# Seven eighths of the attention layer's output product moved into the scan layer's turns, with four transpose banks and another order of transposes

## The chip, the cores and the metric

One core of a Trainium2 chip. The metric is the device time of one execution in microseconds, here the median of three runs. Engines are named as the profile does: PE is TensorE, DVE VectorE, ACT ScalarE, POOL GpSimd, SP SyncE (here it only issues DMAs).

## The reference

```python
# layer 0, for each of 8 batches (1024 rows of 512), 8 heads of 64
xn = _ln(x, ln_w, ln_b)
q = softmax over a head's 64 of (xn @ Wq + bq)
k = softmax over the 1024 rows of (xn @ Wk + bk + (1 - mask) * -1e6)
v = (xn @ Wv + bv) * mask
att = einsum('bnhd,bnhl->bhdl', k, v)
y = einsum('bnhd,bhdl->bnhl', q, att)
hh = _ln(y, ln2_w, ln2_b) * (1 + scale) + shift
x1 = x + silu(hh) @ W_out + b_out
# layer 1: modulated layer norm of x1, rows gathered by an index, a selective
# scan (state size 16, inner width 1024), gated, projected, rows put back
out = x1 + gate * y1
```

The index is below 512 for every row, so the scan layer reads only the first 512 rows (four tiles of 128) of each batch; the other four tiles of x1 only go to the output.

## The kernel before

Two layers run one after the other, each a block in which every engine has its own list of instructions, tied by semaphores. All matmuls are float32.

**The attention layer** (`layer0`) is a pipeline over batches: `body(b, prev, cur, more)` runs for b = 0 to 8, does the first half of batch b and the second half of batch b - 1. TensorE's order in a body is: y product (attention matrix times Q, L672), z transposes (`turn`, L660), K products, V products (`product`, L652), y transposes, Q products, output product (L652, 8 tiles of 128 rows, each four matmuls), Q transposes, K transposes, and the K-V product that gives the attention matrix (L732). Products go round four PSUM banks (`MM_RING`), transposes round two (`TR_RING`); the K-V product has bank 6. `mm_use` and `tr_use` count the uses of the two rings, so that a wait for the fourth or second use before the next can be written as a constant. ScalarE copies z (L749), exponentiates K (L752), turns y into h by Silu (L764), exponentiates Q (L769), copies Q (L774) and multiplies K by the mask (L779). VectorE adds biases, takes maxima and sums, normalizes z and y (L273), and adds the output product to x (`res`, L888); the rows of x1 then go to DRAM. GpSimd takes the power for the norms, adds the output bias to `res` (L796) and shifts Q by its maximum (L806). Body 8 also does three small products (L284) for the modulation of the next layer, and gathers the next layer's first rows. The attention layer ends when the last stores have landed.

**The scan layer** (`layer1`) has eight turns of 32 units, one a batch; a unit is one of 16 states for half of the inner width, and has four blocks (128 blocks a turn). Per block ScalarE makes a decay (L1523) in one of three banks, VectorE scans it (L1863), TensorE transposes a tile of a finished unit into one of two state banks (L1301), and VectorE adds it, scaled, to a sum (L1881); the fourth tile goes by ScalarE (L1539) and an accumulating DMA of GpSimd's (L1742). GpSimd makes a unit's four inputs in one instruction (L1704), in a ring of four, up to four units ahead. All other work of a turn (transposes, the input product `project_in` L1264, the projections L1275 and L1290, the output product L1349, and what ScalarE and VectorE do with each) stands at blocks written out by hand: `XM_AT`, `Z_AT`, `DT_AT`, `Y_AT` and the like give the block n of a turn at which TensorE's list has it. A product is cut into pieces of one or two of its four matmuls, one piece a block (`ROWS_SPLIT`). These jobs go round three work banks; `batch_places` numbers the uses. SP issues the loads in the same written-out way by unit s, among them one of B (`b_wide`, L1079) per unit, three units early. GpSimd's list has gathers, accumulates and the final additions of y by unit. The last batches' stores are arranged apart.

In `both_chunks` stands a second version for indices of 512 and more, which doesn't run here.

## Time and profile before

| | us |
|---|---|
| median of three runs | 3349.63 (3346.01 to 3351.81) |
| the profiled execution's own time | 3346.66 |
| its span, first to last instruction | 3344.9 |
| mean granted clock of TensorE | 0.915 |
| PE busy | 2824.3 (84%) |
| DVE busy | 2437.0 (73%) |
| ACT busy | 1603.8 (48%) |
| POOL busy | 1838.8 (55%) |

The page's second part shows the span in 40 slices of 83.6 us, a digit for the busy tenths. The first fifteen or so are the attention layer, the rest the scan layer: PE stands at 9 in the first and at 7 to 8 in the second, DVE at 3 to 4 and at 9. The granted clock is a share of full speed, and has two levels, 0.5 (1.2 GHz) and 1.0 (2.4 GHz); a number in between is a mean over a stretch. Groups and waits name the tiles as written by the program, out<-in, and in brackets the idle time of the engine just before and what ended it.

### The profile page before, as it was taken

How to read it: one execution, taken by the hardware profiler on the slowest of the kernel's cores; microseconds unless marked ns; L12 is line 12 of the kernel's file. 1: busy time of each engine (PE TensorE's matmuls, PEld its weight loads, DVE VectorE, ACT ScalarE, POOL GpSimd, SP SyncE). 2: the span in 40 equal slices, each digit the busy share in tenths (PEclk: the TensorE clock that was granted, in tenths of full speed). 3: DMA queues.
4: the chain of work that ended last, by engine and by line, in shares of the span. 5: the costliest groups of instructions: out<-in, count | busy, mean ns of one | idle time of the engine just before them, and what ended most of it. 6: DMA issues, size and time to landing. Idle time of an engine off the chain costs nothing. (4 is left out here: it accounts for less than half of the span.)

```text
span 3344.9 us, 33056 instructions
## 1 busy us (share of the span) xinstructions
PE 2824.3 (84%) x11066; PEld 1589.4 (48%) x11066; DVE 2437.0 (73%) x3146; ACT 1603.8 (48%) x2280; POOL 1838.8 (55%) x801
## 2 busy tenths in 40 slices
PE   7999999999999998678788788787787787787874
PEld 3545454545545443435544445445445444444542
DVE  3444444444444343899999999999999999999994
ACT  1122221222212123657767667667667667667561
POOL 0111111111121110878869969969979979879992
PEclk9999999999999999688798898898897898998976
DMA  5002020211102123344345445455456455455563
GB/s 194 7 26 82 0 82 0 82 42 39 56 25 82 38 79 100 81 95 91 93 114 136 112 118 127 114 123 132 108 123 139 105 125 135 101 131 128 131 154 70
DMA packets 216344, 310.97 MB, mean 93 GB/s; under 512 B 19373, under 2 KB 85041, under 8 KB 216202
## 3 DMA queue, kind: packets, MB, share of 16 engines
q1 hardware_dynamic: 164584, 217.10, 20.7%
q0 software_dynamic: 48064, 91.25, 15.6%
q8 instruction: 71, 1.16, 0.1%
q10 hardware_dynamic: 3554, 0.88, 0.1%
q14 instruction: 71, 0.58, 0.1%
HBM read 200.88 MB, written 42.22 MB: 73 GB/s over the span
## 5 line engine op out<-in xcount | busy, mean ns | idle before, releaser
L1704 POOL TENSOR_TENSOR hs<-slots,b_wide 128x2048 f32<-128x2048 f32 x256 | 1230.0, 4818 | 296.6 <-PE bank L1301 233.8
L1863 DVE TENSOR_TENSOR_SCAN hs<-bank,hs 128x512 f32<-128x512 f32 x1024 | 1219.7, 1208 | 51.8 <-ACT bank L1523 47.1
L1301 PE MATMUL bank<-ident,hs 128*128 128x128 f32 x4096 | 729.3, 310 | 401.8 <-DVE acc L1881 298.8
L1523 ACT ACTIVATE bank<-dt,decay 128x512 f32<-128x512 f32 x1024 | 699.0, 691 | 575.4 <-DVE hs L1863 573.6
L1301 PEld LDWEIGHTS bank<-ident,hs 128*128 128x128 f32 x4096 | 534.0, 158 | 915.0 <-DVE acc L1881 333.0
L1881 DVE SCALAR_TENSOR_TENSOR acc<-bank,c_t,acc 128x512 f32<-128x512 f32 x772 | 560.0, 725 | 28.3 <-PE bank L1301 27.4
L1264 PE MATMUL bank<-h_t,w_in 128*128 128x512 f32 x1024 | 512.9, 608 | 1.0 <-ACT h_t L1457 1.0
L1742 POOL DMA_DIRECT2D acc<-scaled x252 | 270.7, 1074 | 25.8 <-DMA acc<-scaled 23.3
L793 POOL TENSOR_TENSOR y_rs<-y_var,mhalf 128x8 f32<-128x8 f32 x8 | 16.0, 2006 | 440.4 <-DVE y_var L267 440.4
L1349 PE MATMUL bank<-w_y,zs 128*128 128x512 f32 x512 | 253.8, 602 | 0.8 <-DVE zs L1982 0.8
L652 PE MATMUL bank<-z_t,w_k 128*128 128x512 f32 x512 | 221.8, 594 | 5.9 <-ACT z_t L749 5.9
L652 PE MATMUL bank<-w_out,h_t 128*128 128x512 f32 x512 | 221.1, 592 | 0.0
L652 PE MATMUL bank<-rows,z_t 128*128 128x512 f32 x512 | 221.1, 592 | 0.0
L652 PE MATMUL bank<-w_v,z_t 128*128 128x512 f32 x512 | 221.0, 592 | 0.0
L801 POOL TENSOR_TENSOR x_rs<-x_var,mhalf 128x8 f32<-128x8 f32 x7 | 11.5, 1647 | 366.9 <-DVE x_var L267 366.9
L1264 PEld LDWEIGHTS bank<-h_t,w_in 128*128 128x128 f32 x1024 | 171.2, 196 | 84.0 <-issue 84.0
L1539 ACT ACTIVATE scaled<-bank,c_t 128x512 f32<-128x512 f32 x252 | 169.9, 674 | 29.6 <-PE bank L1301 15.6
L806 POOL TENSOR_TENSOR qy<-qy,q_top 128x512 f32<-128x512 f32 x64 | 68.8, 1075 | 200.6 <-DVE q_top L876 200.6
L1831 DVE SCALAR_TENSOR_TENSOR slots<-bank,taps,slots 128x511 f32<-128x511 f32 (+2 forms) x192 | 142.1, 740 | 22.7 <-ACT slots L1463 20.1
L652 PEld LDWEIGHTS bank<-z_t,w_k 128*128 128x128 f32 x512 | 96.6, 190 | 126.4 <-issue 124.5
L652 PEld LDWEIGHTS bank<-w_out,h_t 128*128 128x128 f32 x512 | 97.2, 190 | 122.8 <-issue 122.8
L652 PEld LDWEIGHTS bank<-w_v,z_t 128*128 128x128 f32 x512 | 97.3, 190 | 122.5 <-issue 122.5
(157 smaller groups left out, 3127.8 us busy)
## 6 DMA issues: line engine op xcount, KB each, us to landing
b_wide<-b_rows SPq DMA_DIRECT2D x256, 256.0 KB, 3.5
acc<-scaled POOLq DMA_DIRECT2D x252, 256.0 KB, 4.9
w_in<-in_L_cond_W_in SPq DMA_DIRECT2D x128, 256.0 KB, 3.2
z<-in_x SPq DMA_DIRECT2D x8, 2048.0 KB, 8.5
res<-in_x SPq DMA_DIRECT2D x8, 2048.0 KB, 8.7
x_rows<-res SPq DMA_DIRECT2D x7, 2048.0 KB, 7.4
fin<-x_rows SPq DMA_DIRECT2D x48, 256.0 KB, 4.5
out<-fin SPq DMA_DIRECT2D x48, 256.0 KB, 2.0
```

The costliest lines, as they stand in the source:

```text
L652: last = nc.tensor.matmul(out[:, :], stationary(k), moving(k), start=(k == 0), stop=(k == blocks - 1))
L806: nc.gpsimd.tensor_tensor(heads, heads, q_top[:, t, :].unsqueeze(2).to_broadcast([P, HEADS, HEAD]), ALU.add).then_inc(q_shifted, 1)
L1264: last = nc.tensor.matmul(work_bank(place, stage, m)[:, :], w_in[:, m % W_IN_RING, k, :], h_t[:, place.par, k, :], start=(k == 0), stop=(k ...
L1301: last = nc.tensor.transpose(bank[:, j * P:(j + 1) * P], hs[:, slot, j, t * P:(t + 1) * P], ident[:, :])
L1349: last = nc.tensor.matmul(work_bank(place, "out", t)[:, :], zs[:, j, t * P:(t + 1) * P], w_y[:, j, :], start=(j == 0), stop=(j == KI - 1))
L1523: nc.scalar.activation(decay_banks[N % 3][:, :], dt[:, H % 2, j, :], ACT.Exp, scale=g.decay[:, 4 * (H % 2) + j, s:s + 1]).then_inc(da_read ...
L1539: nc.scalar.activation(scaled[:, U % SCALED_RING, t - DVE_TILES, :], state_banks[t % 2][:, :], ACT.Copy, scale=c_t[:, U // UNITS % 2, t, U ...
L1704: nc.gpsimd.tensor_tensor(hs[:, U % RING, :, :], slots[:, H % SLOTS, :, :], b_wide[:, U % B_RING, :].unsqueeze(1).to_broadcast([P, 4, CHUNK]),
L1742: nc.gpsimd.dma_start(acc[:, U // STATE % 2, DVE_TILES:, :], scaled[:, U % SCALED_RING, :, :], accum_op=ALU.add).then_inc(state_pooled, DMA)
L1831: nc.vector.scalar_tensor_tensor(row[:, back:], bank[:, 0:CHUNK - back], w, row[:, back:], ALU.mult, ALU.add).then_inc(empties(place, "xm" ...
L1863: nc.vector.tensor_tensor_scan(block, decay_banks[N % 3][:, :], block, 0.0, ALU.mult, ALU.add).then_inc(scanned, 1)
L1881: nc.vector.scalar_tensor_tensor(part, state_banks[t % 2][:, :], scale, part, ALU.mult, ALU.add).then_inc(summed, 1)
```

## The change

What it does, in both layers:

- In the attention layer the output product stays for tiles 0 to 3 of batches 0 and 1 alone. For all other tiles h is stored to DRAM (`store_h`, four DMAs for each half of a batch, pieces of 512 bytes) and the rows stored as x1 are x plus bias without the product.
- The scan layer's turns 0 to 6 each compute eight of the 56 tiles: SP loads a tile of h (256 KB, ring of three) by `H_IN_AT`, TensorE multiplies in two pieces of two matmuls at the blocks of `W_AT` (the last at block 130, which is block 2 of the next turn), ScalarE copies the bank to SBUF six blocks later (`keep_w`), and GpSimd adds pairs of tiles (512 KB) to x1 in DRAM by an accumulating DMA at the units of `ADD_W_AT` (37 is unit 5 of the next turn). Turn b does the last four tiles of batch b and the first four of batch b + 2; readers of x1 wait for the pair (`w_landed`).
- Transposes of the attention layer go round four banks instead of two, and the K-V product goes to bank 3.
- TensorE's order in a body is now: z transposes, y product, K, V, y transposes, Q, kept output tiles, K transposes, Q transposes, K-V product. ScalarE's K multiplies stand among the exponentials of Q (`K_BEHIND_Q`).
- Bodies 1 to 3 are written out instead of looped, SP's all of them. SP loads the last batch's rows of x at the end of body 7, and GpSimd adds the bias to them there. The small products of body 8 use banks 0 to 3 and wait for the y product's banks to be empty.
- The gather of the scan layer has one x1 tensor for each batch, and GpSimd's eight small index additions go.

```diff
+ROWS_KEPT = NT // 2
+BATCHES_KEPT = 2
+TR_FIRST = {"z": 0, "k": 8, "q": 16}
 TR_USES = 4 * NT
-TR = {"z": 0, "y": 8, "q": 16, "k": 24}
+TR = {"z": 0, "y": 8, "k": 16, "q": 24}
 TR_LAST = {"y": 0}
-MM_RING, TR_RING = 4, 2
+MM_RING, TR_RING = 4, 4
+K_BEHIND_Q = ((), (), (), (), (), (0, 1), (2, 3), (4, 5, 6, 7))
...
+W_RING = 3
+W_TURNS = BATCH - 1
...
+ADD_W_AT = (7, 30, 32, 37)
+H_IN_AT = (-1, 2, 5, 7, 24, 27, 30, 31)
+W_AT = (7, 11, 89, 101, 106, 110, 121, 130)
...
+W_SPLIT = ((0, 1), (2, 3))
...
+def w_tile(w):
+    b, i = w // NT, w % NT
+    if 2 <= i < 6:
+        return (b + 2, i - 2) if b < BATCH - 2 else (BATCH - 1, i + 2)
+    return b, i + 4 if i < 2 else i
+W_TILES = [w_tile(w) for w in range(NT * W_TURNS)]
...
+            for i in range(NT):
+                if n == W_AT[i] and b < W_TURNS:
+                    use(b, "W", i)
+                if n == W_AT[i] - BLOCKS and 0 < b <= W_TURNS:
+                    use(b - 1, "W", i)
...
+    g.x1 = [scratch(f"x1_rows{i}", [SEQ, DIM]) for i in range(BATCH)]
+    g.h_dram = scratch("h_tiles", [BATCH, NT, P, DIM])
...
+        g.w_out = sb("w_out", [P, KD, DIM])
...
+            def store_h(b, half):
+                need(sp, tr_empty, tr_use(b + 1, "y") + 4 * half + 4)
+                for k in range(KD):
+                    sp.dma_start(h_tiles[b, k][:, 4 * half:4 * half + 4, :],
+                                 h_t[:, k, half * 512:(half + 1) * 512].rearrange("p (t c) -> p t c", c=P)).then_inc(h_stored, DMA)
...
-                if prev:
+                if prev and cur:
                     sp.dma_start(res[:, :, :], batch(x_rows, b - 1)).then_inc(res_loaded, DMA)
...
+                if prev:
+                    need(sp, res_ready, NT * b)
+                    if rows_kept(b - 1):
+                        store_rows(b - 1, slice(ROWS_KEPT, NT))
+                    else:
+                        store_rows(b - 1, slice(0, NT))
+                        store_h(b - 1, 0)
+                    store_h(b - 1, 1)
+                    if rows_kept(b - 1):
+                        need(sp, mm_empty, mm_use(b, "W") + ROWS_KEPT)
+                        store_rows(b - 1, slice(0, ROWS_KEPT))
+                    sp.wait_ge(x1_stored, DMA * stores_of_rows(b))
+                if cur and not more:
+                    sp.dma_start(res[:, :, :], batch(x_rows, b)).then_inc(res_loaded, DMA)
                     sp.wait_ge(mm_ready, mm_use(b, "Q") + NT)
...
+                    sp.wait_ge(tr_ready, tr_use(b, "k") + NT)
+                    sp.wait_ge(kv_ready, b + 1)
+                    load_ada(2)
...
                     sp.wait_ge(gate_stored, DMA)
-                    sp.wait_ge(x1_stored, DMA * (b - 1 + NT // 2))
-                elif prev:
-                    need(sp, mm_empty, mm_use(b, "W") + NT)
-                    sp.sem_inc(passed, 1)
-                    sp.dma_start(batch(x1_rows, b - 1), res[:, :, :]).then_inc(x1_stored, DMA)
-
-                    need(sp, x1_stored, DMA * b)
-                    sp.sem_inc(passed, 1)
+                    sp.wait_ge(h_stored, DMA * halves_of_h(b) * KD)
...
+                if cur:
+                    n = tr_use(b, "z")
+                    for half in range(2):
+                        need(pe, z_ready, NT * (b - 1) + 4 * half + 4)
+                        for i in range(KD):
+                            turn(n, 4 * half + i, [z[:, 4 * half + j, i * P:(i + 1) * P] for j in range(4)])
...
+                    need(pe, tr_empty, tr_use(b, "z") + NT)
...
+                    need(pe, mm_empty, mm_use(b, "y") + NT)
...
+                if prev and rows_kept(b - 1):
+                    need(pe, tr_empty, tr_use(b, "y") + 4)
                     pe.wait_ge(w_out_loaded, DMA)
                     n = mm_use(b, "W")
-                    for t in range(NT):
+                    for t in range(ROWS_KEPT):
                         product((n, t), lambda k: h_t[:, k, t * P:(t + 1) * P], lambda k: g.w_out[:, k, :], KD)
                 if cur:
+                    n = tr_use(b, "k")
+                    need(pe, k_exp_ready, KD * b + KD)
+                    for t in range(NT):
+                        turn(n, t, [k_t[:, i, t * P:(t + 1) * P] for i in range(KD)])
                     n = tr_use(b, "q")
                     for half in range(2):
                         need(pe, q_exp_ready, NT * b + 4 * half + 4)
                         for i in range(KD):
                             turn(n, 4 * half + i, [qy[:, 4 * half + j, i * P:(i + 1) * P] for j in range(4)])
-                    n = tr_use(b, "k")
-                    need(pe, k_exp_ready, KD * b + KD)
-                    for t in range(NT):
-                        turn(n, t, [k_t[:, i, t * P:(t + 1) * P] for i in range(KD)])
-
-                    need(pe, tr_empty, n + NT)
+                    need(pe, tr_empty, tr_use(b, "k") + NT)
                     need(pe, att_ready, 2 * b)
+                    need(pe, mm_empty, mm_use(b + 1, "y"))
                     for i in range(KD):
...
                 if prev:
                     need(act, mod_ready, b)
+                    need(act, h_stored, DMA * KD * halves_of_h(b - 1))
...
+                    n = tr_use(b, "k")
+                    need(act, mask_cur_ready, b + 1)
                     for t in range(NT):
                         need(act, q_shifted, NT * b + t + 1)
                         nc.scalar.activation(qy[:, t, :], qy[:, t, :], ACT.Exp).then_inc(q_exp_ready, 1)
+                        for i in K_BEHIND_Q[t]:
+                            need(act, tr_ready, n + i + 1)
+                            nc.scalar.mul(k_exp[:, i, :], bank(i)[:, :], mask_cur[:, i:i + 1]).then_inc(tr_empty, 1)
...
-                    n = tr_use(b, "k")
-                    need(act, mask_cur_ready, b + 1)
-                    for t in range(NT):
-                        need(act, tr_ready, n + t + 1)
-                        nc.scalar.mul(k_exp[:, t, :], bank(t)[:, :], mask_cur[:, t:t + 1]).then_inc(tr_empty, 1)
...
-                    for t in range(NT):
-                        nc.gpsimd.tensor_tensor(res[:, t, :], res[:, t, :], g.out_bias[:, :], ALU.add).then_inc(res_ready, 1)
+                    if cur:
+                        add_out_bias(b)
...
+                if cur and not more:
+                    add_out_bias(b + 1)
...
                     normed(nc, z, x_mv, x_rs, z_ready)
-                if prev:
+                if prev and rows_kept(b - 1):
...
+        def w_landed(eng, b, t):
+            if (b, t) in W_TILES:
+                q = w_pair(b, t)
+                need(eng, w_added[q % 2], DMA * (q // 2 + 1))
...
+            def load_next_h(w):
+                if w < len(W_TILES):
+                    place, i = w_place(w - W_RING)
+                    load_h(w, filled_by(place, "W", i))
...
+                    for i, at in enumerate(H_IN_AT):
+                        if s == at % UNITS:
+                            w = NT * (b - at // UNITS) + i
+                            if w >= W_RING:
+                                load_next_h(w)
...
+            def project_w(place, i, w, ks):
+                if ks[0] == 0:
+                    claimed(pe, place, "W", i)
+                    need(pe, h_loaded[w % W_RING], DMA * (w // W_RING + 1))
+                for k in ks:
+                    last = nc.tensor.matmul(work_bank(place, "W", i)[:, :], h_in[:, w % W_RING, k, :], g.w_out[:, k, :], start=(k == 0), stop=(k == KD - 1))
+                if ks[-1] == KD - 1:
+                    last.then_inc(fills(place, "W", i), 1)
 
...
+            def keep_w(place, i, w):
+                src = filled(place, "W", i)
+                q = w // 2
+                need(act, w_added[q % 2], DMA * (q // 2))
+                nc.scalar.copy(w_part[:, q % 2, w % 2, :], src[:, :]).then_inc(empties(place, "W", i), 1)
 
...
+                        if n == W_AT[i] + 6 and b < W_TURNS:
+                            keep_w(place, i, NT * b + i)
+                        if n == W_AT[i] + 6 - BLOCKS and 0 < b <= W_TURNS:
+                            keep_w(PLACES[b - 1], i, NT * (b - 1) + i)
...
-            def next_rows(b):
-                need(pool, g.rows_loaded, CT * DMA * (b + 1))
-                nc.gpsimd.tensor_scalar(g.idx_in[:, :], g.idx_in[:, :], SEQ, None, ALU.add).then_inc(idx_in_ready, 1)
+                for t in range(CT):
+                    w_landed(pool, b, t)
+                gather_rows(nc, g, g.x1[b][0:CHUNK, :], g.idx_first, 0)
+            def add_w(q, first, second):
+                for place, i in (first, second):
+                    need(pool, *read_by(place, "W", i))
+                b, t = W_TILES[2 * q]
+                nc.gpsimd.dma_start(x1_tiles[b][t:t + 2].rearrange("t p d -> p t d"), w_part[:, q % 2, :, :], accum_op=ALU.add).then_inc(w_added[q % 2], DMA)
 
             def gather_on(it, b, c):
...
+                    for i, at in enumerate(ADD_W_AT):
+                        q = NT // 2 * (b - at // UNITS) + i
+                        if s == at % UNITS and 0 <= q < len(W_TILES) // 2:
+                            add_w(q, w_place(2 * q), w_place(2 * q + 1))
```

## Rows read from the trace of the kernel before

**Rows 1.** The page's part 5, costliest groups: the output product.

```profile
L652 PE MATMUL bank<-w_out,h_t 128*128 128x512 f32 x512 | 221.1, 592 | 0.0
```

**Rows 2.** Windows: us, busy of PE PEld DVE ACT POOL, PEclk, DMA share, GB/s.

```profile
240.00:480.00 240.00, 229.78 (x873) 126.66 (x872) 104.49 (x190) 50.77 (x82) 36.38 (x30) 1.00 0.16 56
...
2000.00:2300.00 300.00, 244.36 (x1048) 141.42 (x1047) 286.24 (x325) 213.86 (x300) 256.70 (x100) 0.90 0.53 123
```

**Rows 3.** Timeline, TensorE, one batch: start us, us, engine, line, operation, tiles, count.

```profile
528.45 1.04 PE L660 MATMUL bank<-ident,qy 128*128 128x128 f32 x8
...
534.13 27.63 PE L652 MATMUL bank<-rows,z_t 128*128 128x512 f32 x64
561.60 27.63 PE L652 MATMUL bank<-w_out,h_t 128*128 128x512 f32 x64
...
589.07 1.04 PE L660 MATMUL bank<-ident,qy 128*128 128x128 f32 x8
...
600.66 7.41 PE L732 MATMUL bank<-values,k_exp 128*128 128x128 f32 x64 [0.78 <-ACT k_exp L779]
...
622.19 18.29 PE L652 MATMUL bank<-z_t,w_k 128*128 128x512 f32 x42 [0.75 <-ACT z_t L749]
```

**Rows 4.** Timeline of the same batches, ScalarE, GpSimd and VectorE.

```profile
446.25 1.27 ACT L779 ACTIVATE k_exp<-bank,mask_cur 128x512 f32<-128x512 f32 x2 [0.26 <-PE bank L660]
...
563.29 1.34 POOL L806 TENSOR_TENSOR qy<-qy,q_top 128x512 f32<-128x512 f32 x1 [2.39 <-DVE q_top L876]
...
563.22 4.44 DVE L273 TENSOR_SCALAR z<-z,x_mv,x_rs 128x512 f32<-128x512 f32 x8
...
564.66 0.63 ACT L769 ACTIVATE qy<-qy 128x512 f32<-128x512 f32 x1 [3.10 <-POOL qy L806]
...
589.70 1.07 ACT L774 COPY q_t<-bank 128x512 f32<-128x512 f32 x2 [24.41 <-PE bank L660]
```

**Rows 5.** Timeline, TensorE, the first batch.

```profile
138.77 1.04 PE L660 MATMUL bank<-ident,qy 128*128 128x128 f32 x8
...
154.30 7.41 PE L732 MATMUL bank<-values,k_exp 128*128 128x128 f32 x64 [0.78 <-ACT k_exp L779]
```

**Rows 6.** Timeline, all engines, the way out of the attention layer.

```profile
1198.17 7.41 PE L732 MATMUL bank<-values,k_exp 128*128 128x128 f32 x64 [0.78 <-ACT k_exp L779]
...
1213.91 7.03 PE L284 MATMUL bank<-z,cond_t 128*8 128x512 f32 x16
...
1230.18 2.97 ACT L764 ACTIVATE h_t<-bank,mod_cur 128x512 f32<-128x512 f32 x4
...
1273.43 0.37 SPq L630 DMA_DIRECT2D x_rows<-res  x1
1276.70 1.66 DVE L2022 TENSOR_SCALAR d_diag<-ident,cols 128x128 f32<-128x128 f32 x8 [3.29 <-PEq L524]
```

**Rows 7.** Groups by line, 1400 to 3200 us: busy, mean ns, idle before and releaser.

```profile
L1704 POOL TENSOR_TENSOR hs<-slots,b_wide 128x2048 f32<-128x2048 f32 x237 | 1139.9, 4823 | 228.5 <-PE bank L1301 227.2
...
L1863 DVE TENSOR_TENSOR_SCAN hs<-bank,hs 128x512 f32<-128x512 f32 x946 | 1126.9, 1208 | 43.0 <-ACT bank L1523 43.0
...
L1881 DVE SCALAR_TENSOR_TENSOR acc<-bank,c_t,acc 128x512 f32<-128x512 f32 x710 | 515.0, 725 | 24.4 <-PE bank L1301 24.3
...
L1742 POOL DMA_DIRECT2D acc<-scaled x237 | 253.3, 1069 | 25.1 <-DMA acc<-scaled 23.3 <-issue 1.6
...
L1475 ACT COPY zs<-bank 128x512 f32<-128x512 f32 x64 | 37.2, 581 | 12.3 <-PE bank L1264 12.3
```

**Rows 8.** Windows and timeline in the first part of a scan turn.

```profile
2336.20:2400.00 63.80, 48.25 (x223) 32.67 (x223) 58.66 (x70) 45.44 (x66) 59.57 (x27) 0.79 0.53 118
...
2380.43 5.52 POOL L1704 TENSOR_TENSOR hs<-slots,b_wide 128x2048 f32<-128x2048 f32 x1
...
2392.29 2.32 DVE L1863 TENSOR_TENSOR_SCAN hs<-bank,hs 128x512 f32<-128x512 f32 x2
```

**Rows 9.** DMA issues, 1400 to 3300 us: count, KB each, us to landing.

```profile
acc<-scaled POOLq DMA_DIRECT2D x248, 256.0 KB, 4.9
```

More of the change, by code:

```diff
@@ L784, in _, with add_out_bias @@
         def _(pool):
+            def add_out_bias(stores):
+                need(pool, res_loaded, DMA * stores)
+                for t in range(NT):
+                    nc.gpsimd.tensor_tensor(res[:, t, :], res[:, t, :], g.out_bias[:, :], ALU.add).then_inc(res_ready, 1)
             def body(b, prev, cur, more):
@@ L1798, in both_chunks @@
             def both_chunks():
+                for q in range(len(W_TILES) // 2):
+                    add_w(q, (w_first, 2 * q), (w_first, 2 * q + 1))
+                pool.wait_ge(rows_copied, DMA * BATCH)
                 def body(b):
```

168 lines of the change are left out of this document (99 added, 69 removed).

## The prediction

> **What bounds the kernel now.** I read the busy time by stages first [rows 2]. The kernel has two halves with different limits. In the attention half TensorE is busy 229.8 of 240 us at the full clock while VectorE is busy 104.5, so there time is TensorE's work. In the scan half VectorE is busy 286 of 300 us and TensorE 244, so there TensorE work is mostly hidden and VectorE's waits are the price list. The output product is 512 matmul records, 221.1 us [rows 1], 27.6 us a batch, and it stands in the first half. Then I read TensorE's order of work in one batch [rows 3] with the short steps of the other engines around it [rows 4], the first batch [rows 5], the way out of the attention half [rows 6], and for the scan half the idle time ahead of each group [rows 7].
>
> A change under 0.2% (7 us) can't be told from none here.
>
> **Part 1: what leaves the attention half.** 56 of 64 output tiles leave it. Call E the end of the Q products; in [rows 3] it is 561.60. Before: the output product fills 27.5 us, then Q and K transposes with two banks, and the K-V product starts at 600.66, E+39.1.
>
> After, in a batch with no output product, K transposes come at once (K was exponentiated long before). ScalarE's line decides: bank 0 is readable 0.63 us after a transpose starts (589.07 to 589.70) [rows 3, 4]; two K multiplies take 1.27, one exponential 0.63, two Q copies 1.07 [rows 4]. So E+0.6; K0, K1 to 1.9; exponential 6 to 2.5; K2, K3 to 3.8; the last exponential, whose input GpSimd ends at E+3.0 (563.29 + 1.34), to 4.4; K4 to K7 to 7.0; the first four Q copies to 9.1. TensorE's last Q turn waits for the fourth of these (four banks), takes 0.52 and lets the K-V product start at about E+10. Gain 29.1 us. VectorE's two sets of eight passes (normalizing z, 4.4 us from 563.22 [rows 4], then the Q sums, about as long) end near E+11, ahead of the K-V product's end at E+17.4, and cost nothing; were they late, they would hold the attention matrix and so the y product.
>
> Where half the product is kept (two batches) 13.7 us of this stay: gain 15.4. The first batch has no output product: 15.5 us between its Q products and its K-V product [rows 5] become 10, gain 5.5.
>
> From the K-V product's end (608.07) to the K product's start (622.19) are 14.1 us [rows 3]: a wait for the attention matrix, the y product (64 records like the K-V product's, 7.4), z turns, a wait for the last copy. With z turns first the first wait lies behind them and the last behind the y product: about 4.2 + 7.3 = 11.5. Gain 2.6. The y turns took 5.7 us (528.45 to 534.13). With four banks the last one starts after the fourth Silu, 0.64 + 4 x 0.74 [rows 6], so 4.1: gain 1.5. Both seven times.
>
> The way out: 71.1 us from the last K-V product's end (1198.17 + 7.41) to the first VectorE work of the scan half (1276.70) [rows 6]. After: 8.4 to the end of the y product, 0.9 for VectorE's last read of a bank (a new wait; such a read is 0.73 in [rows 7]), 14.1 for two modulation products, 2.2 to the first Silu (1213.91 + 14.1 to 1230.18). TensorE's y turns end near 29.1; then 0.7 for the small turns, 7.0 for the third product, 1.2 to the gate's store, and from the issue of a last store to the next half 3.3 as before (1273.43 to 1276.70): 41.3. Gain 29.8. The new stores of h are ready first: last Silu at 31.6, four issues of 0.4, 4.9 to land [rows 9], 38.1.
>
> Sum: 5.5 + 2 x 15.4 + 5 x 29.1 + 7 x 4.1 + 29.8 = **240.3 us** off the first half, 193.5 of it moved matmuls (7/8 of 221.1), the rest waits. Bounds: without any gain from order and banks only the matmuls go, 193; if TensorE's own 16 turns of 0.52 (8.3 us) set the K-V product's start, 1.7 more in each of eight batches, 254. I stay at 240 because every step of it has a row.
>
> The added transfers of this half (2 MB of h a batch, in pieces of 512 bytes) go beside it: no engine waits for them within 100 us. If that cover went, the wait would be ScalarE's before Silu. Unrolled bodies and a later load of the last rows of x cost nothing: POOL and SP have nothing else then.
>
> **Part 2: what the scan half pays.** Seven turns of 32 units each take eight tiles. Per turn:
> - TensorE: 27.6 us of matmuls at full clock, in pieces of 1.7 us. VectorE now waits for TensorE 24.3 us in 7.4 turns (237 units, 32 a turn) [rows 7], 3.3 a turn. A piece adds its 1.7 to a block of VectorE's of 1.9 (a scan 1.21, an add 0.73), with two state banks between the engines, so it hides at full clock where TensorE idled. The granted clock was 0.79 in the first 64 us of a turn [rows 8], so partly the 1.2 GHz level, and three tiles stand there: six pieces of 3.4 us. Bounds: below zero, -2 (clock comes up, existing waits shrink), above +10 (six pieces 1.7 us longer). I take +1.5, nearest to today's waits.
> - ScalarE: eight copies of 0.58 [rows 7] = 4.6 us. VectorE waits for ScalarE 43.0/7.4 = 5.8 us a turn, in bursts; six of the eight copies fall where ScalarE idles, two beside the table loads. Bounds 0 and 4.6; I take +1.0.
> - GpSimd: four accumulating DMAs to DRAM of 512 KB. No row has that transfer; an accumulating one of 256 KB into SBUF takes 1.07 us of issue [rows 7] and 4.9 to land [rows 9]. Three of four are issued at the start of a turn, where GpSimd is busy 59.6 of 63.8 us [rows 8]. Its lead over VectorE is smallest there: input 8 ends at 2385.95 (2380.43 + 5.52), its scan starts at 2392.29, 6.3 us [rows 8]. Three issues take 3.2; each can delay the next accumulate by up to 4.9. Bounds 0 and 3.2 + 14.7 - 6.3 = 11.6; I take +1.5, because the lead covers all issues and half the delays.
> - SP: eight loads of 256 KB a turn, each waiting for a matmul three tiles earlier; behind it wait loads of B, issued three units (over 20 us) early. Nothing.
>
> Together 4.0 a turn, **+28 us**; bounds -14 and +183, the upper only if all ends meet.
>
> On the DMA the Trainium skill (DMA: Bandwidth & Descriptors, Anatomy of one DMA) gives a GpSimd-issued transfer 2.0 us plus bytes over 436 GB/s. By it 256 KB are 2.6 us, where this trace has 4.9; for 512 KB it would say 3.2, and then the GpSimd term would be nothing. The measured one decides.
>
> Sum against the profiled execution: 3346.66 - 240.3 + 28 = 3134.4. That execution is 3.0 us under the median of the three runs (3349.63), so **3137 us**.
>
> **Rivals.**
> A. GpSimd becomes the bound at the start of each turn (0.10). For it: the lead of 6.3 us. Against: 228 us of its idle time in the rest. Near the bound of 11.6 a turn instead of 1.5: +71, 3208.
> B. The added matmuls bring TensorE's clock up where it was 0.79, and the scan half isn't longer: -1 a turn, 3137 - 28 - 7 = 3102 (0.14). For it: over all stages of a turn the clock is 0.90 [rows 2], so it is higher where more full-size matmuls stand. Against: the low stretch also holds small matmuls and waits that stay. The Trainium skill (TensorE: Matmul & The Clock Gate, What's actually happening) says the gate is released by sustained activity, which is this mechanism; the trace agrees in that low stretches stand where TensorE waits.
> C. The attention half falls short (0.06): another engine's line shows up once the output product is gone, and only the 193 us of matmuls go: 3137 + 47 = 3184.
> D. Slower than before (0.03): accumulating into DRAM reads and writes it, and each of the four waits in GpSimd's queue. GpSimd idles 228.5/7.4 = 31 us a turn; the gain is 240.3/7 = 34 a turn; so it decides from (31 + 34)/4 = 16 us each. At four times the 4.9 us [rows 9] (twice the bytes, twice the traffic) it is 19.6: (78 - 31) x 7 = +329, so 3349.6 - 240.3 + 329 = 3438.
> E. A queue order or a wait undoes the move, and the time stays within 0.2% (0.01).
>
> **How the numbers follow.** The forecast has 0.66. Its own range is a first-half gain of 230 to 250 with 1 to 9 us a turn in the second: 3107 to 3183. The range takes in B's 3102 and most of C: **3098 to 3190**, leaving out A's upper part, D and E, and half of B's tail. Faster by over 0.2%: all but D and E, 0.96; same 0.01; slower 0.03.
>
> **What would show it.** In the profile after: the attention half ends (first VectorE work of the scan half) near 1036 instead of 1277. The K-V product starts about 10 us after the last Q product, 24 in two batches; from one K product's start to the next are 29.1 + 4.1 = 33.2 us less than before. The output product has 64 records at its old line and 448 at a new one. A turn of the scan takes 4 us more; VectorE's idle time ahead of scans and sums grows from 9.1 us a turn to about 13, by ScalarE and TensorE. Wrong would be: a wait for GpSimd's inputs ahead of the scans (A), a granted clock near 1.00 throughout and no longer turns (B), TensorE idle over 3 us ahead of the K-V or y product (C), GpSimd waiting for its new DMAs (D).

## The result and the profile after

| | before | after |
|---|---|---|
| median, us | 3350.07 (3346.01 to 3351.81) | 3134.01 (3131.16 to 3136.52) |
| the profiled execution's own time | 3346.66 | 3136.52 |
| its span | 3344.9 | 3134.7 |
| first VectorE work of the scan half | 1276.70 | 1019.67 |
| scan half (the rest of the span) | 2068.2 | 2115.0 |
| mean granted clock | 0.915 | 0.942 |

The medians are over four executions each; the 3349.63 above was over three of the four before. The scan half is the span less the start of its first VectorE work, the attention half what stands ahead of it.

The ratio is 0.9355 [0.934, 0.937]: 6.45% faster. The forecast was 3137. The sum is right to 3 us, but that is luck: it is made of two errors that cancel. The attention half came out 257.0 us shorter (forecast 240.3), the scan half 46.8 us longer (forecast 28).

The group of the moved matmuls on the page after (line, engine, operation, tiles, count, busy, mean ns, idle before and its releaser):

```profile
L1399 PE MATMUL bank<-w_out,h_in 128*128 128x512 f32 x448 | 234.2, 649 | 1.3 <-ACT dt L1647 1.3
```

The output product has 448 records at its new line [rows 1]. Its mean is 649 ns where the old line had 592 at the full clock: some of the moved matmuls run in stretches of low clock.

TensorE's timeline of one batch after, the stretch that answers to [rows 3]:

```profile
510.75 2.78 PE L719 MATMUL bank<-ident,k_t 128*128 128x128 f32 x24
...
519.65 7.31 PE L793 MATMUL bank<-values,k_exp 128*128 128x128 f32 x64
526.79 3.66 PE L719 MATMUL bank<-ident,z 128*128 128x128 f32 x32
530.29 7.31 PE L737 MATMUL bank<-att,q_t 128*128 128x128 f32 x64
537.43 27.63 PE L711 MATMUL bank<-z_t,w_k 128*128 128x512 f32 x64
...
592.37 4.13 PE L719 MATMUL bank<-ident,qy 128*128 128x128 f32 x32
596.34 27.63 PE L711 MATMUL bank<-rows,z_t 128*128 128x512 f32 x64
...
650.50 4.89 PE L711 MATMUL bank<-z_t,w_k 128*128 128x512 f32 x11
```

The Q products end at 510.75. The K-V product starts 8.9 us later (519.65), the y product follows the z transposes with no wait, and from K product to K product are 650.50 - 537.43 = 113.07 us where 148.77 stood before.

VectorE's groups over five turns of the scan half, first before, then after (the shape group of `slots` and smaller ones left out). The windows run from one early operation of a turn (the first of `h_t`) to the same one five turns on, 1230.03 and 1267.31 us, so a turn went from 246.0 to 253.5 us:

```profile
L1863 DVE TENSOR_TENSOR_SCAN hs<-bank,hs 128x512 f32<-128x512 f32 x640 | 762.6, 1208 | 30.5 <-ACT bank L1523 30.5
L1881 DVE SCALAR_TENSOR_TENSOR acc<-bank,c_t,acc 128x512 f32<-128x512 f32 x481 | 349.0, 726 | 18.5 <-PE bank L1301 18.4
...
L334 DVE TENSOR_SCALAR var<-mv 128x4 f32<-128x4 f32 x5 | 10.9, 2178 | 0.2
...
L340 DVE SCALAR_TENSOR_TENSOR shift<-mv,rs 128x4 f32<-128x4 f32 x5 | 2.2, 437 | 1.9 <-POOL rs L320 1.9
```

```profile
L2029 DVE TENSOR_TENSOR_SCAN hs<-bank,hs 128x512 f32<-128x512 f32 x641 | 763.9, 1208 | 28.0 <-ACT bank L1673 28.0
L2047 DVE SCALAR_TENSOR_TENSOR acc<-bank,c_t,acc 128x512 f32<-128x512 f32 x481 | 349.5, 727 | 38.2 <-PE bank L1435 37.2 <-issue 0.2
...
L371 DVE SCALAR_TENSOR_TENSOR shift<-mv,rs 128x4 f32<-128x4 f32 x5 | 22.3, 4467 | 4.2 <-POOL rs L351 4.2
...
L365 DVE TENSOR_SCALAR var<-mv 128x4 f32<-128x4 f32 x5 | 2.8, 560 | 0.2
```

Three things moved. VectorE's waits for TensorE ahead of the sums went from 18.4 to 37.2 us, 3.8 us a turn. Its waits for ScalarE ahead of the scans went from 30.5 to 28.0. And `shift`, an operation on four numbers a partition, went from 437 to 4467 ns. Together with `var` (2178 to 560 ns) and the wait ahead of it (1.9 to 4.2) that is (20.1 - 8.1 + 2.3)/5 = 2.9 us a turn, of which the prediction has nothing.

The cause of the longer `shift` can be read off GpSimd's and VectorE's timelines at that point. Before, at one turn's start, GpSimd:

```profile
2356.50 1.68 POOL L320 TENSOR_TENSOR rs<-var,mhalf 128x4 f32<-128x4 f32 x1
2358.26 0.25 POOL L1671 TENSOR_SCALAR idx_in<-idx_in 128x8 int32<-128x8 int32 x1
2358.59 4.54 POOL L1704 TENSOR_TENSOR hs<-slots,b_wide 128x2048 f32<-128x2048 f32 x1
```

and VectorE:

```profile
2358.21 0.16 DVE L340 SCALAR_TENSOR_TENSOR shift<-mv,rs 128x4 f32<-128x4 f32 x1 [0.56 <-POOL rs L320]
```

After, GpSimd, and then VectorE:

```profile
2373.45 1.66 POOL L351 TENSOR_TENSOR rs<-var,mhalf 128x4 f32<-128x4 f32 x1
2374.48 5.09 POOL L1866 TENSOR_TENSOR hs<-slots,b_wide 128x2048 f32<-128x2048 f32 x1
```

```profile
2375.14 4.46 DVE L371 SCALAR_TENSOR_TENSOR shift<-mv,rs 128x4 f32<-128x4 f32 x1 [1.63 <-POOL rs L351]
```

Before, the small index addition stood between the power (`rs`) and the making of a unit's inputs, and VectorE's shift, released by the power, ran beside it in 0.16 us. With the addition gone, GpSimd goes straight on into the inputs, and shift ends with that instruction, at 2379.6. The Trainium skill (SBUF — State Buffer, Who interferes with whom) says that a VectorE instruction with two SBUF inputs contends with a GpSimd instruction that reads SBUF, by a lock held for the whole instruction, and that the one that starts second blocks; `shift` has two such inputs (`mv`, `rs`), and the rows agree.

### The profile page after: what moved, and what is told of

It reads as the page before. It is cut to its first block and busy times, and to the rows that moved or that the text cites. A ratio compares the mean times of both kernels' runs of the same rounds, so it can differ in the third digit from the quotient of the medians.

```text
span 3134.7 us, 32596 instructions
## 1 busy us (share of the span) xinstructions
PE 2724.0 (87%) x11066; PEld 1530.8 (49%) x11066; DVE 2404.3 (77%) x3090; ACT 1615.8 (52%) x2336; POOL 1868.2 (60%) x821
## 5 line engine op out<-in xcount | busy, mean ns | idle before, releaser
L1435 PE MATMUL bank<-ident,hs 128*128 128x128 f32 x4096 | 681.1, 294 | 310.4 <-DVE acc L2047 240.8
L1435 PEld LDWEIGHTS bank<-ident,hs 128*128 128x128 f32 x4096 | 507.1, 150 | 848.0 <-DVE acc L2047 319.5
L2047 DVE SCALAR_TENSOR_TENSOR acc<-bank,c_t,acc 128x512 f32<-128x512 f32 x772 | 560.9, 727 | 62.7 <-PE bank L1435 60.6
L1399 PE MATMUL bank<-w_out,h_in 128*128 128x512 f32 x448 | 234.2, 649 | 1.3 <-ACT dt L1647 1.3
L868 POOL TENSOR_TENSOR x_rs<-x_var,mhalf 128x8 f32<-128x8 f32 x7 | 11.5, 1647 | 330.8 <-DVE x_var L298 330.8
L813 ACT ACTIVATE k_t<-k_t,k_top 128x1024 f32<-128x1024 f32 x32 | 36.8, 1149 | 250.0 <-DVE k_top L915 250.0
L1997 DVE SCALAR_TENSOR_TENSOR slots<-bank,taps,slots 128x511 f32<-128x511 f32 (+2 forms) x192 | 142.1, 740 | 22.4 <-ACT slots L1613 19.9
```

The source lines that it names most:

```text
L1399: last = nc.tensor.matmul(work_bank(place, "W", i)[:, :], h_in[:, w % W_RING, k, :], g.w_out[:, k, :], start=(k == 0), stop=(k == KD - 1))
L1435: last = nc.tensor.transpose(bank[:, j * P:(j + 1) * P], hs[:, slot, j, t * P:(t + 1) * P], ident[:, :])
L1997: nc.vector.scalar_tensor_tensor(row[:, back:], bank[:, 0:CHUNK - back], w, row[:, back:], ALU.mult, ALU.add).then_inc(empties(place, "xm" ...
L2047: nc.vector.scalar_tensor_tensor(part, state_banks[t % 2][:, :], scale, part, ALU.mult, ALU.add).then_inc(summed, 1)
```

## The experiments

Each median is over four executions; the kernel before was timed beside each set of runs and stayed within 3350.1 to 3350.8. "Scan half" is that of the profiled execution, as in the table above. It moves by up to 5 us between kernels whose scan layers are the same (2110.6 in e9, 2114.8 in e10, 2115.7 in e5), so a difference of 4 us in it is no more than a hint.

| run | median, us | scan half starts | scan half |
|---|---|---|---|
| changed kernel | 3134.01 | 1019.67 | 2115.0 |
| e1_idx_add | 3115.79 | 1019.84 | 2095.0 |
| e2_no_w | 3110.29 | 1017.10 | 2088.1 |
| e3_small_mm | 3133.13 | 1017.35 | 2111.8 |
| e4_all_kept | 3313.61 | 1222.30 | 2088.1 |
| e5_after_again | 3135.62 | 1020.35 | 2115.7 |
| e6_small_copies | 3134.18 | 1019.05 | 2115.0 |
| e7_small_adds | 3127.84 | 1018.90 | 2108.4 |
| e8_norm_on_gpsimd | 3107.12 | 1017.01 | 2087.5 |
| e9_two_banks | 3177.05 | 1063.81 | 2110.6 |
| e10_old_order | 3178.62 | 1062.57 | 2114.8 |
| e11_norm_no_w | 3077.22 | 1018.73 | 2054.6 |
| e12_norm_small_mm | 3096.27 | 1017.13 | 2074.4 |

**e1_idx_add.**

```diff
                         if s == 5:
                             rows_rsqrt(nc, g, b + 1)
+                            nc.gpsimd.tensor_scalar(g.idx_in[:, :], g.idx_in[:, :], SEQ, None, ALU.add).then_inc(idx_in_ready, 1)
```

> The changed kernel with GpSimd's small index addition (0.25 us) put back right behind its power for the norms; everything else as in the changed kernel. Theory 1 (the removed addition is what lengthened VectorE's small operation): without it GpSimd goes from the power straight into the 4.5 us making of a unit's inputs, and VectorE's shift, which takes the power's result, lasts as long as that instruction (4.46 us instead of 0.44). Then shift is back at about 0.4 us, var at about 2.2, the wait for the power smaller, 2.4 to 2.9 us less a turn, seven times: 17 to 20 us under the changed kernel, 3114 to 3117 us. Theory 2 (the two engines collide whatever stands between, or another wait takes the place): shift stays at 4 us, or the time it frees comes back as waits for TensorE, and the time stays at 3134 within 3 us.

Measured 3115.79, 18.2 us under the changed kernel; theory 1. GpSimd and VectorE's shift in the turn shown above (timelines), and shift's group over all of the scan half's turns:

```profile
2364.00 0.25 POOL L1915 TENSOR_SCALAR idx_in<-idx_in 128x8 int32<-128x8 int32 x1
2364.34 4.54 POOL L1866 TENSOR_TENSOR hs<-slots,b_wide 128x2048 f32<-128x2048 f32 x1
```

```profile
2363.95 0.16 DVE L371 SCALAR_TENSOR_TENSOR shift<-mv,rs 128x4 f32<-128x4 f32 x1 [1.51 <-POOL rs L351]
```

```profile
L371 DVE SCALAR_TENSOR_TENSOR shift<-mv,rs 128x4 f32<-128x4 f32 x7 | 4.7, 678 | 4.9 <-POOL rs L351 4.9
```

The seven shifts took 25.4 us in the changed kernel and take 4.7 here. The scan half is 20.0 us shorter, little else having moved: an instruction that computes nothing that is used makes the kernel 0.6% faster. Not expected was that `var` stays at 792 ns; it isn't the addition that decides it.

**e2_no_w.**

```diff
-W_TURNS = BATCH - 1
+W_TURNS = 0
...
-                for w in range(W_RING):
-                    load_h(w, None)
```

> The changed kernel without the moved work in the scan layer: no loads of h, no products, copies and accumulates of the 56 tiles (x1 of those rows is x plus bias alone). Theory 1 (the moved work costs the scan half about 4.6 us a turn, and the other 2.9 of the 7.5 us are the lengthened shift, which stays here): 7 x 4.6 = 32 us under the changed kernel, 3102 us, turns of 249 us. Theory 2 (all 7.5 us of a turn are the moved work): turns of 246 us and 3134 - 52 = 3082 us.

Measured 3110.29 (3107.04 to 3117.34), 24 to 25 us under the changed kernel, closer to theory 1 (3102) than to theory 2 (3082). The scan half is 26.9 us shorter, and VectorE's seven shifts still take 25.5 us. So the scan half's 46.8 us split into 19.9 for the removed index addition (2088.1 less the 2068.2 of before) and 26.9 for the moved work, where the prediction had 28 for the moved work alone. The 26.9 are rather too low a price: `var` takes 14.0 us in this run and 5.5 in the changed kernel, so part of the gain was lost to GpSimd again. e11 prices the moved work with `var` and `shift` out of the way.

**e3_small_mm.**

```diff
-    last = nc.tensor.matmul(work_bank(place, "W", i)[:, :], h_in[:, w % W_RING, k, :], g.w_out[:, k, :], ...
+    last = nc.tensor.matmul(work_bank(place, "W", i)[:, 0:64], h_in[:, w % W_RING, k, :], g.w_out[:, k, 0:64], ...
```

> The changed kernel with the scan layer's output product on 64 of its 512 columns (loads, waits, copies and accumulates stay; the sums are incomplete). Theory 1 (of the moved work only the length of its matmuls costs, as VectorE's waits for TensorE's transposes, 3.7 us a turn more than before): about 3134 - 26 = 3108 us, VectorE's wait ahead of the sums falls from 7.5 to 3.7 us a turn. Theory 2 (without full matmuls the granted clock falls back from 0.95 to about 0.87 and gives the gain back): half of it or less, 3120 us or more. Theory 3 (copies and accumulates are what costs): 3134 us, unchanged.

Measured 3133.13, 1 to 2.5 us less, which is no clear gain. Of the moved matmuls' busy time, 234.2 us, 77.7 are left. Read alone this says that the length of the matmuls costs nothing, but the waits say otherwise. VectorE's waits in the whole span (engine, what waited, for what: us, times, longest), of the changed kernel:

```profile
DVE acc L2047 <- PE bank L1435: 60.6, 63, 3.1
...
DVE hs L2029 <- ACT bank L1673: 43.9, 45, 3.4
```

and of this run:

```profile
DVE hs L2029 <- ACT bank L1673: 51.0, 45, 3.4
DVE acc L2047 <- PE bank L1435: 32.3, 38, 2.8
```

The waits for TensorE fell by 28.3 us, to near the 27.4 of the kernel before. What came in their place is 7.1 us of waits for ScalarE, and `var`, which now runs into GpSimd's instructions:

```profile
L365 DVE TENSOR_SCALAR var<-mv 128x4 f32<-128x4 f32 x7 | 19.6, 2801 | 0.2
```

against 5.5 us. The shifts take 27.5 us and the wait ahead of them 5.9, against 25.4 and 4.2. That is 14.1 + 2.1 + 1.7 us, and with 7.1 for ScalarE 25.0 of the 28.3. The mean granted clock is 0.918 in place of 0.942, so theory 2's condition holds as well; e12 tells these apart.

**e4_all_kept.** The output product entirely in the attention layer, the scan layer without it, all else of the change kept (the last batch's eight tiles wait until the small products' banks have been read).

```diff
-ROWS_KEPT = NT // 2
-BATCHES_KEPT = 2
+ROWS_KEPT = NT
+BATCHES_KEPT = BATCH
...
-W_TURNS = BATCH - 1
+W_TURNS = 0
...
+                    if not cur:
+                        pe.wait_ge(ada_folded, 5)
```

> Only the other part of the change: four transpose banks, the new order of transposes and K multiplies and the written-out bodies, with the whole output product kept in the attention layer and nothing of it in the scan layer. Theory 1 (the prediction's split: 193.5 of the attention half's gain are moved matmuls, 46.8 are order, banks and the way out): 47 us less in the attention half than before; the scan half keeps the lengthened shift (7 x 2.9 = 20 us), so 3350 - 47 + 20 = 3323 us, K product to K product about 6 us shorter than the 148.77 of before. Theory 2 (order and banks bring something only once the output product is away, since it covered ScalarE's work): attention half 0 to 15 us shorter, 3355 to 3370 us.

Measured 3313.61, ratio 0.9896 [0.988, 0.9913]. The scan half starts at 1222.30, 54.4 us earlier than before (expected 47), and it is 19.9 us longer by the shift: theory 1. Its shifts take 25.4 us, as in the changed kernel. Order and banks pay with the product in place too:

```profile
590.38 27.63 PE L703 MATMUL bank<-z_t,w_k 128*128 128x512 f32 x64
...
705.56 2.78 PE L711 MATMUL bank<-ident,k_t 128*128 128x128 f32 x24
...
714.46 7.31 PE L787 MATMUL bank<-values,k_exp 128*128 128x128 f32 x64
...
732.25 27.63 PE L703 MATMUL bank<-z_t,w_k 128*128 128x512 f32 x64
```

From K product to K product 141.87 us: 6.9 less than the 148.77 of before. The K-V product starts 8.9 us after the TensorE work ahead of it, as in the changed kernel. The rest of the change, from here to 1019.67, is 202.6 us for 56 tiles, 3.6 us a tile, where the moved matmuls are 3.45. Most of the 9 us between is in the y transposes, which take 5.3 us a batch here and 4.0 in the changed kernel.

**e5_after_again** has no edit.

> The changed kernel itself, so that its profile and times stand beside the other runs on the same chip. Expected 3134 us within 4, and VectorE's scan at the 1216 ns that the experiments on this chip show instead of 1208.

Measured 3135.62 (3133.95 to 3137.78), so the control repeats. The scan's mean is 1207 ns here, and not the 1217 of e1 to e4; the starts of scans and sums follow each other at 1.13 and 0.65 us in both, so this is no difference in pace.

**e6_small_copies.**

```diff
-                nc.scalar.copy(w_part[:, q % 2, w % 2, :], src[:, :]).then_inc(...)
+                cols = DIM if w < 4 else 16
+                nc.scalar.copy(w_part[:, q % 2, w % 2, 0:cols], src[:, 0:cols]).then_inc(...)
```

> The changed kernel with ScalarE's copies of the output product cut to 16 of 512 columns (from the fifth tile on; the rest added to x1 is stale). Theory 1 (the copies delay ScalarE's decays; they carry most of what is left of the 24 to 27 us that leaving all moved work out gave back): 10 to 20 us under the changed kernel, VectorE's wait for decays about 2 us a turn less. Theory 2 (the copies stand where ScalarE idles, or another wait takes the place): within 5 us of 3134.

Measured 3134.18, nothing; theory 2. The length of ScalarE's copies is hidden.

**e7_small_adds.**

```diff
-                nc.gpsimd.dma_start(x1_tiles[b][t:t + 2].rearrange("t p d -> p t d"), w_part[:, q % 2, :, :], accum_op=ALU.add)...
+                nc.gpsimd.dma_start(x1_tiles[b][t:t + 2].rearrange("t p d -> p t d")[0:8], w_part[0:8, q % 2, :, :], accum_op=ALU.add)...
```

> The changed kernel with each accumulating DMA into x1 on 8 of 128 partitions (32 KB instead of 512 KB; the sums are incomplete). Theory 1 (the big transfers delay GpSimd's other accumulates and by them the inputs and VectorE): 5 to 20 us under the changed kernel. Theory 2 (GpSimd's lead covers them, as no scan waits for GpSimd's inputs): within 4 us of 3134.

Measured 3127.84, 7 to 8 us less; theory 1, but not by its path. No scan waits for GpSimd's inputs but the first, 4.7 us in either kernel. The group of shift:

```profile
L371 DVE SCALAR_TENSOR_TENSOR shift<-mv,rs 128x4 f32<-128x4 f32 x7 | 19.2, 2737 | 0.0
```

against 25.2 and a wait of 3.3 in the control: that is 9.3 us. GpSimd came to its power sooner (in one turn it starts 2.8 us behind VectorE's last `mv`, which was 6.5 in the changed kernel), no shift had to wait for it, and the collision got milder. So most of the transfers' price also came through the lock.

**e8_norm_on_gpsimd.** VectorE's var and shift are done by GpSimd around its power (needs between them as for any two operations that depend on each other).

```diff
+def rows_norm_on_gpsimd(nc, g, it):
+    need(nc.gpsimd, g.aggr, CT * it + CT)
+    nc.gpsimd.tensor_scalar(g.var[:, :], g.mv[:, :, 1], EPS, None, ALU.add).then_inc(g.var_ready, 1)
+    need(nc.gpsimd, g.var_ready, it + 1)
+    nc.gpsimd.tensor_tensor(g.rs[:, :], g.var[:, :], g.mhalf[:, 0:CT], ALU.pow).then_inc(g.rs_ready, 1)
+    need(nc.gpsimd, g.rs_ready, it + 1)
+    nc.gpsimd.tensor_tensor(g.shift[:, :], g.mv[:, :, 0], g.rs[:, :], ALU.mult).then_inc(g.shift_ready, 1)
+    need(nc.gpsimd, g.shift_ready, 2 * it - 1)
+    nc.gpsimd.tensor_scalar(g.shift[:, :], g.shift[:, :], -1.0, None, ALU.mult).then_inc(g.shift_ready, 1)
...
-                            rows_rsqrt(nc, g, b + 1)
+                            rows_norm_on_gpsimd(nc, g, b + 1)
```

> The changed kernel with VectorE's two small operations of the norm (var, shift) done by GpSimd itself, right before and behind its power, in the scan layer's turns. VectorE then has neither the 4.2 us of shift and 0.5 us of var nor the 0.7 us wait for the power, 5.4 us a turn. Theory 1 (what VectorE is spared, the turn is spared): 7 x 5.4 = 38 us under the changed kernel, 3096 us. Theory 2 (beyond what the put-back index addition gave, 18 us, TensorE's and ScalarE's lists set the pace and their waits take the place, or GpSimd's extra 3 us a turn cost as much): 3110 to 3118 us.

Measured 3107.12, ratio to the kernel before 0.9274 [0.9259, 0.929], the fastest complete version: 27 to 28 us under the changed kernel, between the theories. On GpSimd the three added operations take 0.20 to 0.25 us each. VectorE is spared the shifts, `var` and the waits ahead of them, 25.4 + 5.5 + 4.4 = 35.3 us; 28 of them reach the end. Its waits show where some of the rest went:

```profile
DVE acc L2060 <- PE bank L1448: 64.9, 61, 2.9
...
DVE hs L2042 <- ACT bank L1686: 47.7, 45, 3.4
```

8.1 us more than in the changed kernel, in waits for the other two engines.

**e9_two_banks.**

```diff
-MM_RING, TR_RING = 4, 4
+MM_RING, TR_RING = 4, 2
```

> The changed kernel with the transposes of the attention layer on two banks again, its new order kept. Theory 1 (four banks bring, per batch, 1.6 us at the y transposes, about 1.1 at the Q transposes, since the last one then waits for the sixth copy of Q and not the fourth, and up to 1 at the z transposes): 3 to 3.7 us a batch, eight batches, 24 to 30 us over 3136, 3160 to 3166 us; y transposes near 5.6 us instead of 4.0. Theory 2 (ScalarE's line alone sets these stretches and the banks change nothing): 3136 us within 4.

Measured 3177.05, 41 to 43 us more, above theory 1's range. In one batch (TensorE's timeline):

```profile
527.47 1.04 PE L719 MATMUL bank<-ident,k_t 128*128 128x128 f32 x8
528.85 1.23 PE L719 MATMUL bank<-ident,k_t 128*128 128x128 f32 x8 [0.34 <-ACT k_exp L836]
...
538.74 7.31 PE L793 MATMUL bank<-values,k_exp 128*128 128x128 f32 x64
```

The K-V product starts 11.3 us after the Q products (8.9 with four banks), the y transposes take 5.7 (4.0), and from the K-V product to the K product are 19.2 (17.8): 2.4 + 1.8 + 1.4 = 5.6 us a batch, not 3 to 3.7. With two banks TensorE waits for ScalarE after each pair.

**e10_old_order.** Four banks, the old order: y product ahead of the z transposes, Q transposes ahead of K, K multiplies behind the copies of Q.

```diff
-TR = {"z": 0, "y": 8, "k": 16, "q": 24}
+TR = {"z": 0, "y": 8, "q": 16, "k": 24}
...
-                        for i in K_BEHIND_Q[t]:
-                            need(act, tr_ready, n + i + 1)
-                            nc.scalar.mul(k_exp[:, i, :], bank(i)[:, :], mask_cur[:, i:i + 1]).then_inc(tr_empty, 1)
```

> The changed kernel with the old order of transposes (y product ahead of z, Q ahead of K, ScalarE's K multiplies behind the copies of Q), four banks kept. Theory 1 (with Q first the K multiplies, 8 x 0.61 us, all stand behind the last copy of Q, so the K-V product starts about 13 us after the last Q product instead of 9; and the wait for the attention matrix is no longer covered by z transposes, 2.6 us): 4 x 6 batches without output product, 4 x 2 or less with, and 7 x 2.6: 40 to 50 us over 3136, 3176 to 3186 us. Theory 2 (TensorE's own transposes fill the stretch in either order): under 10 us.

Measured 3178.62, 43 to 45 us more; theory 1. The same stretch of its timeline:

```profile
520.77 1.91 PE L719 MATMUL bank<-ident,qy 128*128 128x128 f32 x16
...
533.03 7.41 PE L792 MATMUL bank<-values,k_exp 128*128 128x128 f32 x64 [1.66 <-ACT k_exp L840]
541.50 7.41 PE L731 MATMUL bank<-att,q_t 128*128 128x128 f32 x64 [1.05 <-DVE att L968]
...
553.52 27.73 PE L711 MATMUL bank<-z_t,w_k 128*128 128x512 f32 x64 [1.12 <-ACT z_t L809]
```

The K-V product starts at 12.3 us, and the two waits around the y product (1.05 and 1.12, those of the kernel before) are back: 3.4 + 2.7 = 6.1 us a batch.

**e11_norm_no_w**: the edits of e8 and e2 together.

> The kernel with var and shift on GpSimd (3107.12 us) and without the moved work in the scan layer (no loads, products, copies, accumulates of the 56 tiles). VectorE then never meets GpSimd's lock in its norm, so this is the price of the moved work by itself. Theory 1 (the price is VectorE's waits for TensorE, 3.7 us a turn over the kernel before): 26 us less, 3081 us. Theory 2 (with the norm away VectorE's waits at blocks 9 to 17 shrink anyway, or GpSimd's added operations now set the start of a turn): the price is under 15 us, 3092 us or more.

Measured 3077.22 (3073.17 to 3085.89), 29.9 us under e8, 32.9 in the scan half; theory 1. VectorE's waits:

```profile
DVE hs L2040 <- ACT bank L1684: 53.0, 49, 3.6
...
DVE acc L2058 <- PE bank L1446: 29.0, 36, 1.9
```

The waits for TensorE fall by 35.9 us against e8 and are again those of the kernel before (27.4); ScalarE takes 5.3 back.

**e12_norm_small_mm**: the edits of e8 and e3 together.

> The kernel with var and shift on GpSimd (3107.12 us) and the scan layer's output product on 64 of 512 columns, all else kept. In the same cut of the changed kernel VectorE's waits for TensorE fell by 27 us in six turns and the time by 3 alone, since var then met GpSimd's lock for 14 us more. Theory 1 (that was the lock: without it the length of the matmuls shows its price): 20 to 30 us less, 3077 to 3087 us. Theory 2 (the lower granted clock or ScalarE takes it back whatever the lock): less than 8 us, 3100 us or more.

Measured 3096.27, 10.9 us under e8, 13.1 in the scan half: between the theories. VectorE's waits:

```profile
DVE hs L2042 <- ACT bank L1686: 60.8, 50, 3.5
DVE acc L2060 <- PE bank L1448: 35.3, 47, 2.9
```

29.6 us less for TensorE, 13.1 more for ScalarE. With the lock out of the way the same cut that brought 1 to 2.5 us in e3 brings 11, so the lock did take much of it; the other part goes to waits for ScalarE's decays. Why those grow when TensorE's matmuls get shorter isn't settled; that the granted clock is lower (0.921 against 0.944) is no explanation by itself, since e11 has 0.914 and 19.8 us less. Nor does the cut take all of the matmuls away: with an eighth of the columns a third of their busy time is left (234.2 us in the changed kernel).

```profile
L1412 PE MATMUL bank<-w_out,h_in 128*128 128x64 f32 x448 | 73.0, 293 | 1.3 <-ACT dt L1660 1.3
```

Of the 30 to 33 us that the moved work costs on this kernel (e11), e12 explains 11 to 13. No run takes out the loads of h alone, and with the lock away none takes out the copies or the accumulates, so how the rest divides stays open.

## Why the prediction was right, point by point

**Attention half, 240.3 forecast, 257.0 measured.** The split into matmuls and waits holds: e4 has 54.4 us without any moved matmul (46.8 forecast), and moving them brought 202.6 (193.5 forecast). The terms:

- K-V product at E+10: measured E+8.9, eight times, 9 us of the difference. The prediction laid ScalarE's durations end to end, while in the trace neighbours overlap by about 0.1 us, so the first Q copy starts at 517.01, E+6.3 and not E+7.0; and 9.1 + 0.5 was rounded up to 10. ScalarE's line doesn't quite decide, either: TensorE's own sixteen transposes fill all but 0.8 us of the 8.9 (waits of 0.27 and 0.53).
- y transposes at 4.1: measured 3.97.
- K-V product's end to K product 11.5: measured 537.43 - 526.96 = 10.5, seven times. The y product has no wait before or behind it; both covers worked as argued.
- From K product to K product: 33.2 less forecast, 35.7 measured, nearly the sum of the three above.
- Way out 41.3: measured 39.1 (980.56 to 1019.67). The y transposes end 28.6 us in (forecast 29.1) and the third product at 36.1 (36.8). The gate's store is issued 0.8 us behind that and not 1.2, and the next half starts 2.2 us behind the store where the prediction took 3.3 from another store:

```profile
1017.46 0.30 SPq L695 DMA_DIRECT2D gate_rows<-k_t  x1
...
1019.67 1.66 DVE L2187 TENSOR_SCALAR d_diag<-ident,cols 128x128 f32<-128x128 f32 x8 [0.33 <-PEq L556]
```

- The first K product starts at 57.54 (56.27 before), but with the same attention layer it starts at 58.19 in e5 and at 54.86 in e8, so this isn't shown to be an effect of the change.
- No engine's wait is put down to the new stores of h. No run tests the written-out bodies alone.

The three steps inside a batch came out 1.1, 0.1 and 1.0 us too careful, all in the same direction. Of the banks the prediction named 1.5 us a batch; e9 says 5.6. The rest was inside its E+10 and 11.5, which were worked out with four banks, so the sum had it and the text gave the banks too little credit. Without the banks the attention half gains 212.9 us (e9), without the order 214.1 (e10), each about 20 over the 193.5 of the matmuls, where both together give 63.5: most of it comes only with both.

**Scan half, +28 forecast, +46.8 measured.** Of this the moved work is 26.9 (e2), or 32.9 when priced on the kernel without the lock (e8 less e11); the forecast's 28 lies between. By terms:

- TensorE +1.5 a turn: the waits ahead of the sums rose by 3.8 a turn. Where they stand was right in kind, the start of the turn. TensorE in the changed kernel there:

```profile
2356.04 3.12 PE L1399 MATMUL bank<-w_out,h_in 128*128 128x512 f32 x4
2359.00 0.60 PE L1435 MATMUL bank<-ident,hs 128*128 128x128 f32 x4
2359.44 1.88 PE L1399 MATMUL bank<-w_out,h_in 128*128 128x512 f32 x4
```

and VectorE beside it:

```profile
2361.87 0.75 DVE L2047 SCALAR_TENSOR_TENSOR acc<-bank,c_t,acc 128x512 f32<-128x512 f32 x1 [2.51 <-PE bank L1435]
```

These are the two pieces of the tile that `W_AT` puts at block 130, the last of the turn before, which falls on block 2 of this one. They (3.12 us at partly low clock, then 1.88) stand between the transposes that VectorE's sums need, and one sum waits 2.51 us. There is one such wait in each of the seven turns that have this tile, 2.5 to 3.1 us long, 19.4 of the 60.6 us together (added up from the timeline); the kernel before has none there. The term was sized from the mean idle time of a whole turn; at the start of a turn TensorE has no such slack. It was mis-sized: 3.8 instead of 1.5, inside its bounds.
- ScalarE +1.0: measured about 0 (e6, 0.7 us in all). Its copies are hidden.
- GpSimd +1.5: measured 1.0 (e7), by another path, the lock.
- SP: forecast at nothing. No run takes its loads of h out alone, so this isn't tested.

**The step that failed** isn't a term of the sum but a missing one. The section on the change says that GpSimd's eight small index additions go; the prediction gave them no sentence. Removing 0.25 us of GpSimd's work cost 20 us (e1), because its place in GpSimd's queue was what let VectorE's shift through. The rows for it were in the trace of before: a shift of 0.16 us right beside the index addition, and a `var` of 2.2 us on average, the same collision one step earlier. There VectorE's `var` starts inside one of GpSimd's unit inputs and ends with it, at 2353.0:

```profile
2348.03 4.93 POOL L1704 TENSOR_TENSOR hs<-slots,b_wide 128x2048 f32<-128x2048 f32 x1
```

```profile
2350.08 2.91 DVE L334 TENSOR_SCALAR var<-mv 128x4 f32<-128x4 f32 x1
```

So 18.8 us too much cost in the scan half, 19.9 of them this missing term less 1.1 on the moved work, met 16.7 us too little gain in the attention half, and the sum came out right by luck.

**Rivals.** A: no scan beyond the first waited for GpSimd's inputs, but GpSimd did decide at the turn's start, through the lock and not through the lead of 6.3 us. B: its condition came true (granted clock 0.95 over five turns against 0.87) and its effect didn't: turns are 7.5 us longer, and e11, without the moved work, is the fastest of all at 0.914. By the rule of the Trainium skill (TensorE: Matmul & The Clock Gate, What's actually happening) the clock should have come up, and in the trace it did. C: the attention half gave more than 193. D: GpSimd's new accumulates take 1.8 us of issue (mean) and land in 8.9 us (median), far from the 16 from which it would decide. By the Trainium skill (DMA: Bandwidth & Descriptors, Anatomy of one DMA) 512 KB would be an estimated 3.2 us, and the trace doesn't agree; twice the 4.9 us of the 256 KB transfer [rows 9] was the better guide. E: the time fell by far more than 0.2%.

## What to carry to other kernels

An instruction that looks free may be the gap in which another engine's operation gets its turn: before deleting or moving one on GpSimd, look at what VectorE starts right after it, and look in the trace for small VectorE operations that last as long as a GpSimd instruction. Where VectorE is the bound, let GpSimd do the tiny operations around its own result; that was worth 27 to 28 us here, 18 of which the put-back index addition brings as well. When a cut of one cost brings nothing, compare the waits and not only the times: in e3 28 us of waits went away and 25 came back elsewhere, so costs have to be priced on a kernel from which the other effect is gone.

## What was unexpected

- A VectorE operation on 128 x 4 numbers takes 0.16 us in the median of seven turns with a 0.25 us instruction at the right place of GpSimd's queue, and 4.46 us without it.
- The prices don't add up: cutting matmul length, copies and accumulates one by one gives 3.9, 0.7 and 7.3 us of scan half against e5, 11.9 together, while leaving all of the moved work out gives 27.6.
- 448 matmul records of 64 columns keep TensorE busy for 73 to 78 us where those of 512 take 234, so e3 and e12 remove two thirds of the moved matmuls' time and not seven eighths.
- Normalizing y for the last batch took 3.7 us after and 11.3 before, when GpSimd added the bias to the rows beside it, from 1222.34 to 1233.44. That GpSimd's additions are the cause is read from these two traces; no run tests it.
